# The first feed-forward's weights dequantised inside the first attention's steps, and value latents by transposes

## The reference

```
wq = qw[:, None, :] >> shifts[None, :, None] & NIB
wq = wq.reshape(-1, qw.shape[1]).astype(jnp.float32)
zq = qz[:, :, None] >> shifts[None, None, :] & NIB
zq = zq.reshape(qz.shape[0], -1).astype(jnp.float32) + 1.0
return sc[g_idx] * (wq - zq[g_idx])
```

## Time and profile before

| | us |
|---|---|
| median of 3 runs (2582.13 to 2592.98) | 2584.31 |
| the profiled execution | 2582.9 |
| its span | 2580.8 |
| its mean granted TensorE clock | 0.951 of full |

### The profile page before, as it was taken

How to read it: one execution, slowest core, us unless ns; L and a number is a source line. 1 busy time by engine, 2 the same in 40 slices (tenths; PEclk the granted TensorE clock), 3 DMA queues, 4 the chain that set the end, 5 groups by cost and what they waited for, 6 DMA issues and landing times. The chain is left out here.

```text
span 2580.8 us, 44531 instructions
## 1 busy us (share of the span) xinstructions
PE 2364.9 (92%) x14333; PEld 2053.6 (80%) x14333; DVE 1773.9 (69%) x3131; ACT 1459.6 (57%) x3978; POOL 1568.7 (61%) x1320
## 2 busy tenths in 40 slices
PE   8899999993899889999899999998999999987998
PEld 7788888882488778888788888887888888875886
DVE  3566656665923269888788888888888888972232
ACT  1466656661043346667666667666676666664432
POOL 2555555630044277887787878878778878751442
PEclk8899999996599989999999999999999999997999
DMA  2101010101000021110111111101101111003000
GB/s 96 31 23 41 23 41 18 33 1 41 0 1 1 29 64 35 47 55 17 57 45 36 47 42 43 44 29 52 54 24 55 37 42 48 23 5 139 1 17 17
DMA packets 41352, 93.75 MB, mean 36 GB/s; under 512 B 4836, under 2 KB 6760, under 8 KB 39808
## 3 DMA queue, kind: packets, MB, share of 16 engines
q1 hardware_dynamic: 41092, 90.55, 10.9%
HBM read 79.78 MB, written 10.75 MB: 35 GB/s over the span
## 5 line engine op out<-in xcount | busy, mean ns | idle before, releaser
L1095 POOL TENSOR_TENSOR a_nf_acc<-a_nf_acc,a_nf_term 128x512 f32<-128x512 f32 (+1 forms) x416 | 588.6, 1415 | 143.0 <-ACT a_nf_term L1189 72.6
L1575 POOL TENSOR_TENSOR f_w_lo<-WGU,f_w_hi 128x512 fp32r<-128x512 f32 x88 | 114.9, 1307 | 347.8 <-ACT f_w_hi L1591 347.6
L1149 ACT ACTIVATE a_probs<-bank,a_dip 128x128 f32<-128x128 f32 (+1 forms) x512 | 208.3, 419 | 199.5 <-DVE a_dip L1430 199.5
L1158 ACT ACTIVATE a_probs<-a_probs,a_share 128x128 f32<-128x128 f32 (+1 forms) x512 | 192.4, 464 | 61.5 <-DVE a_share L1436 61.5
L1076 POOL TENSOR_TENSOR a_qk_lo<-a_straight,a_qk_hi 128x512 fp32r<-128x512 f32 (+1 forms) x160 | 194.3, 1216 | 47.5 <-ACT a_qk_hi L1135 47.5
L63 PE MATMUL bank<-a_wo_hi,a_ot_hi 128*128 128x512 f32 x512 | 212.3, 415 | 0.0
L365 POOL TENSOR_TENSOR a_straight<-a_straight,a_crossed 128x512 f32<-128x512 f32 x64 | 82.4, 1288 | 212.9 <-DVE a_crossed L718 212.9
L1500 DVE TENSOR_SCALAR a_nf_term<-a_nf_unit 128x512 f32<-128x512 f32 (+1 forms) x288 | 203.6, 751 | 3.4 <-DVE a_nf_unit L1483 0.6
L1441 DVE TENSOR_TENSOR a_pt_lo<-bank,a_pt_hi 128x384 fp32r<-128x384 f32 x256 | 140.9, 550 | 93.8 <-ACT a_pt_hi L1166 93.2
L65 PE MATMUL bank<-a_wo_hi,a_ot_lo 128*128 128x512 f32 x512 | 201.3, 393 | 0.0
L64 PE MATMUL bank<-a_wo_lo,a_ot_hi 128*128 128x512 f32 x512 | 201.0, 392 | 0.0
(11 more groups left out here) (247 smaller groups left out, 8633.0 us busy)
## 6 DMA issues: line engine op xcount, KB each, us to landing
a_raw<-in_l_o SPq DMA_DIRECT2D x64, 256.0 KB, 2.6
a_raw<-in_l_vk SPq DMA_DIRECT2D x32, 384.0 KB, 3.1
a_raw<-in_l_ql SPq DMA_DIRECT2D x32, 320.0 KB, 2.9
a_raw<-in_l_ou SPq DMA_DIRECT2D x32, 288.0 KB, 2.8
n_codes<-coded_w SPq DMA_DIRECT2D x8, 1056.0 KB, 13.1
a_raw<-in_l_nr SPq DMA_DIRECT2D x16, 384.0 KB, 3.0
a_nf_raw<-in_w_nf SPq DMA_DIRECT2D x24, 256.0 KB, 2.6
coded_w<-a_nf_acc SPq DMA_DIRECT2D x24, 256.0 KB, 2.0
```

The lines of the kernel that those rows point to most:

```text
L1095: pool.tensor_tensor(acc, left, nf_term[:, i % CODE_RING, 0:w], ALU.add).then_inc(nf_added, 1)
L1149: act.activation(probs[:, n % 2, col:col + keys], bank[:, at:at + keys], ACT.Exp, bias=dip[:, n % 2, i:i + 1], accum_out=total[:, n % 2, i ...
L1158: ins = act.activation(cell, cell, ACT.Copy, scale=share[:, n % 2, i:i + 1])
```

## The change

`gptq_block` is gone. What it did is cut into 66 pieces of 256 columns (44 of WGU, 22 of WD), which are further units "G" of the attention's ring. Step 3 of each group has one, steps 4 to 11 two each; the last group ends with 15 of them. A piece on TensorE is two matmuls with 256 columns: one with 32 rows (one-hot by zero points) and one with 64 rows (one-hot by the scales' high and low parts, stacked). VectorE makes the nibbles of the step's pieces, then their differences, then their products, each at the end of its step, behind everything else; SyncE stores each result (128 KB) to DRAM. Three result slots are used in turn.

The tables are made on VectorE in steps 0 to 3 of group 0, one of four parts in each; SyncE then (`n == 3`) waits for the tables and loads the packed words over the space that some of their sources used, and the first piece waits for that load. Scales arrive early; the zero words and group numbers are loaded after the latents, into the space of the latents' tables.

`ffn_block` has 33 new loads on SyncE, issued when the block begins, from DRAM to WGU and WD; ScalarE waits for a unit's three loads before it splits the unit's first part.

The groups are all written out (no loop), so no wait is on a register.

The latents come before W0 and W1 now, in the order: four query units, W0, W1, two key units, W2, W3, the value latents, A0, A1. The value latents are eight transposes (64 rows to 64 columns) of the key latents that VectorE has read out of PSUM, instead of 96 matmuls.

```diff
+def dequantised_at(g, n):
+    each = 1 + 2 * PAIRS * 2
+    at = {3: range(0, 1), **{4 + i: range(1 + 2 * i, 3 + 2 * i) for i in range(2 * PAIRS)}}.get(n, range(0))
+    return [("G", each * g + i) for i in at if each * g + i < DEQ_UNITS]
...
         def groups(eng, body):
             body(0, True, False)
-            with eng.Fori(1, L0_GROUPS - 1) as g:
+            for g in range(1, L0_GROUPS - 1):
                 body(g, False, False)
             body(L0_GROUPS - 1, False, True)
...
+                    if first and n == 3:
+                        sp.wait_ge(q_ready, 1)
+                        sp.dma_start(packed, q["q_gu"]).then_inc(q_landed, 16)
+                        sp.dma_start(packed_d, q["q_d"]).then_inc(q_landed, 16)
+                    for _, i in dequantised_at(g, n):
+                        store(i)
...
+                    elif name[0] == "G":
+                        pe.wait_ge(q_ready, 1)
...
+                        pe.matmul(bank[:, 0:PART], hot[0:32, rows:rows + P], table[0:32, cols:cols + PART],
+                                  start=True, stop=True)
+                        last_ = pe.matmul(bank[:, PART:2 * PART], hot[64:P, rows:rows + P], table[64:P, cols:cols + PART],
+                                          start=True, stop=True)
...
+            def value_latents():
+                pe.wait_ge(lat_low, 1)
                 for t in range(TT):
-                    for k in range(KT):
-                        last = product(pe, banks[6][:, t * LAT:(t + 1) * LAT], XT[:, k, t * P:(t + 1) * P],
-                                       lat_w[:, k, QL:QL + LAT], k == 0, k == KT - 1)
+                    h, col = divmod(t, TT // 2)
+                    if col == 0:
+                        pe.wait_ge(lat_crossed, h + 1)
+                    last = pe.transpose(banks[0][:, t * LAT:(t + 1) * LAT], lat_straight[0:LAT, h, col * P:(col + 1) * P],
+                                        ident[0:LAT, 0:LAT])
...
+                def dequantise(names):
+                    for name in names:
+                        i = name[1]
+                        dve.wait_ge(q_landed, 32)
...
+                        wait(dve, differed, i - 1)
+                        dve.tensor_scalar(nib[:, i % 2, :], src, shift, 15, ALU.logical_shift_right, ALU.bitwise_and)\
+                           .then_inc(nibbled, 1)
+                    for name in names:
...
+                        dve.wait_ge(nibbled, i + 1)
+                        dve.wait_ge(unit_done, number[name] + 1)
+                        wait(dve, dequantised, i - 1)
+                        dve.tensor_tensor(diff[:, i % 2, :], nib[:, i % 2, :], bank[:, 0:PART], ALU.subtract)\
+                           .then_inc(differed, 1)
+                    for name in names:
...
+                        dve.wait_ge(differed, i + 1)
+                        wait(dve, q_stored[i % 3], 16 * (i // 3))
+                        dve.tensor_tensor(parked[:, i % 3, :], diff[:, i % 2, :], bank[:, PART:2 * PART], ALU.mult)\
+                           .then_inc(dequantised, 1)
+                        dve.wait_ge(dequantised, i + 1)
+                        dve.sem_inc(ring_free, 1)
...
+                    if first and n < 4:
+                        (zeros_out, scales_high, scales_low, groups_hot)[n]()
+                    dequantise([name for name in units if name[0] == "G"])
...
                 src, hi, _ = cells(u, i)
+                if source and u < FT:
+                    act.wait_ge(loaded[u], 48)
                 wait(act, (gated, upped, downed)[i], u - 1)
...
+            if source:
+                for m in range(FT):
+                    for i in range(2):
+                        sp.dma_start(WGU[:, :, (i * FT + m) * P:(i * FT + m + 1) * P], source[0][i * FT + m])\
+                          .then_inc(loaded[m], 16)
+                    sp.dma_start(WD[:, m, :], source[1][m]).then_inc(loaded[m], 16)
```

More of the change, by code:

```diff
@@ L264, in span @@
         def span(kind, first, last, g):
[L266 to L275, removed]
+            names = {"pieces": lambda k: [x for _, x in l0_pieces(k == 0, k == L0_GROUPS - 1)], "units": l0_units,
+                     "roped": lambda k: [u for u in l0_units(k) if u[0] == "A"],
+                     "plain": lambda k: [u for u in l0_units(k) if u[0] in "WB"]}[kind]
+            base = sum(len(names(k)) for k in range(g))
+            at = {x: base + i for i, x in enumerate(names(g))}
+            return at, at
         def groups(eng, body):
             body(0, True, False)
-            with eng.Fori(1, L0_GROUPS - 1) as g:
+            for g in range(1, L0_GROUPS - 1):
                 body(g, False, False)
@@ L307, in body, with grouped @@
+            def grouped(tensor):
+                return tensor.partition_broadcast(P)
             def body(g, first, last):
                 at, place = span("pieces", first, last, g)
[L309 to L318, removed]
+                names = l0_pieces(first, last)
+                for p, (_, name) in enumerate(names):
+                    if p < 6 and first:
+                        load(name, at, g)
+                if first:
+                    sp.wait_ge(lat_ready, 1)
+                    sp.dma_start(q_down[64:P, :], q["scale"][:, 2 * C:NQ]).then_inc(q_late, 16)
+                    sp.dma_start(word_wide, q["z_gu"]).then_inc(q_late, 16)
+                    sp.dma_start(word_down, q["z_d"]).then_inc(q_late, 16)
+                    sp.dma_start(q_index[:, 0:KT * P], grouped(q["g_gu"])).then_inc(q_late, 16)
+                    sp.dma_start(q_index[:, KT * P:NG], grouped(q["g_d"])).then_inc(q_late, 16)
+                for n in range(-1, L0_STEPS):
+                    for p, (_, name) in enumerate(names):
+                        asked = names[p - 2][0] if p >= 2 else -1
+                        if asked == n and not (first and p < 6):
+                            load(name, at, g)
+                    if first and n == 3:
[4 more added lines that the diff above has]
+                        store(i)
@@ L527, in piece_ready @@
                     else:
-                        names = [x for _, x in l0_pieces(False, False)]
-                        left = len(names) - names.index((kind, i, h, 1))
-                        pe.wait_ge(split, pieces[("OU", 1, 0, 0)] - left + 1)
+                        pe.wait_ge(split, span("pieces", g == 1, False, g - 1)[0][(kind, i, h, 1)] + 1)
                 def project(name):
@@ L1554, in ffn_block @@
         UNITS = 2 * FT
+        loaded = [sem(f"loaded{m}") for m in range(FT)] if source else None
         late = range(TT - 2, TT)
```

382 lines of the change are left out of this document (206 added, 176 removed).

## The result

The changed kernel took 2603.8 us in the median of 20 runs (one of them, at 7702 us, was disturbed and is left out of every comparison), the kernel before 2587.8 us. The ratio is 1.0058, 95% interval 1.0042 to 1.0074: slower by 0.6%, some 15 us. The forecast was 2590.0 with a range of 2555 to 2612.

The account below looks back on a forecast made before the run. It took a first-attention chain without slack (A, rotation, low part, transposes, low part, next A) as deciding. From 2582.9 us, -95.3 + 4.7 - 9.8 + 86.6 + 18.6 + 2 = +6.8 gave 2590, range 2555 to 2612.

Parts of the forecast that it names:

- The steps: First attention's steps with pieces: nibbles wait for GpSimd, so the next projection A is late; +2.7 us typically, +86.6 together.
- The first rival: Steps with pieces: nibbles don't take turns with GpSimd, 23 steps at 1.4 us, -30, giving 2560; chance 0.22.
- Block: Between attention and feed-forward: the separate dequantisation goes, -95.3 us.
- feed-forward start: Feed-forward's beginning: ScalarE, and TensorE behind it, wait for the first three loads; +4.7 us (2 to 8).
- tables: Steps 0 to 3 of group 0: VectorE's table work takes 17.3 us, plus 9 (3 to 12) for turns with GpSimd.
- load: Start of the first attention: VectorE's first piece waits for the packed words, 9 us (8 to 13).
- the start's gain: Start of the kernel: the new order brings the first scores to 54.5 us, 18.8 earlier (15 to 20).
- The clock: TensorE's half clock behind pauses: +6 us at the start, +2 in the last group.
- The second rival: Steps with pieces: the clock falls behind TensorE's pauses; in each of 31 steps +124 us, 2714; chance 0.09.
- The loop: First attention's group loop written out: jump-back pause, half clock and longer loop steps go; -9.8 us.

Follow-up runs that it names:

- e2: Changed kernel with GpSimd's low part of the rotated query waiting until the step's nibbles are made; 2562.1 us, ratio 0.9914.
- e1: Changed kernel with the nibble instructions issued earlier in the step, where VectorE idles and GpSimd is nearly idle; 2547.3 us, ratio 0.9855.
- e3: Changed kernel with the output addition (and the measurement behind it) moved behind the step's dequantisation; 2593.7 us, ratio 1.0032.
- e7: Kernel before with only the written-out groups of the first attention and the new start order with transposes; 2548.3 us, ratio 0.9862.
- e10: e1 with the output addition moved behind the step's dequantisation as well; 2535.9 us, ratio 0.9811.
- e11: e1 with the wide packed words loaded a step earlier and the feed-forward's start reordered; 2536.7 us, ratio 0.9822.
- e12: e1 with both zero-point products ahead of both scale products in each pair of pieces; 2538.7 us, ratio 0.9825.
- e6: Kernel before with only the first attention's group loop written out; 2563.9 us, ratio 0.9921.
- e15: Kernel before with the group loops of both attentions written out; 2566.7 us, ratio 0.9929.

## Why the prediction came out as it did

**The steps: right.** Turn-taking with GpSimd at the nibbles, product and bank free late, A late: 9.87 instead of the 10.0 said, a pair of nibbles 1.64 (1.3 to 1.5 was said for the second alone), pause 0.90 instead of 1.1 to 1.4. e2 took the one cause away and got 2562, e1 2547. The first rival, the same without turn-taking, took 23 steps at 1.3 off, 30 us, to 2560; its condition was not met. When e2 met it, those steps were 1.03 shorter each, 24 us, and the rest of its 42 was mostly clock (the table under e3). That it stands at 2562, near the 2560, is chance.

**Block, feed-forward start, tables, load: right** within 2 us each, by the table at the head; e7 confirms the start's gain of 15.

**The clock: the step that failed.** The prediction held that TensorE's pauses of 1.1 to 1.4 in each step are too short to matter ("about 1.08 it held 1.0", and "1.4 is nearer to 1.08") and gave +2 for the last group and +6 for the start. It judged a single pause by the earlier trace rows, where none stood beside it. What the intervals behind steps 4 to 12 have beyond their usual length adds up to 37 us (8.3, 11.4, 5.7 and 11.4 in the four groups; 1 of it is the additions' own), where 9 were said, 8 for the clock and 0.8 for the measurements: the term was 28 too small. The full steps, 0.13 shorter than said, gave 4 back. The same sum, additions and measurements included, is 16 in e1's trace, 18 in e10's and e11's and 31 in e12's, all without the 0.90: it fell, by how much differs from trace to trace, and what makes the clock fall stays open. The second rival had the mechanism, but all or nothing, with 124 us for every step; it should have been a term of the sum, for a part of the steps.

**The loop: right at its place, and blind beyond it.** −9.8 was said and −11.6 measured in the first attention. That the second attention would gain 10 or 11 us with nothing in it changed, no row of before told; it hid the clock's term. Without it the changed kernel would have stood near 2615, outside the range. That the sum came within 8 us of the profiled run is luck: errors of 28 and 12 us had opposite signs.

## What to carry to other kernels

Ahead of adding work to an engine with slack, lay its form beside what the other engine on its memory port does at that moment: two instructions moved ahead of one other in VectorE's queue, or one wait on GpSimd, were worth 56 and 42 us. When an added wait makes TensorE pause in every step, price the half clock as a term of its own, as a range: the same row of pauses held the clock in one group here and lost it in the next, so neither one row of before nor one trace after tells it. And measure each part of a change by itself: here two parts brought 37 us, and the dequantisation in the steps cost 51, and only the nibbles' place and what followed from it turned that round.

## What was not expected of the hardware

- A loop written out in one block shortened another block by 10 us (e6), at the turn of that block's own loop; writing out that one too brought nothing, and its groups took 4.4 us more in all (e15).
- A lone 256-column product costs TensorE 0.31 us where the row range changes each time, and 0.19 of it goes with the change (e12).
- The same pause in the same surroundings, 1.07 us with 0.90 in the steps around, was followed by a clock of 0.57 over 6 us in group 1 and by 1.00 in group 2 of the changed kernel; a pause of 0.93 did both in e12.
- GpSimd's subtraction ran beside VectorE's PSUM-reading difference with neither longer (e2), where beside the nibbles the pair took 1.64 instead of 0.61.
